# Attention whose score and maximum tiles share PSUM banks, with two maximum tiles directly in front of the value product

## The chip, the cores and the metric

One NeuronCore of a Trainium2 chip runs the whole program. The metric is the device time of one execution in microseconds (us); lower is better. Three executions of the kernel before gave 2846.3, 2852.3 and 2852.42 us, a median of 2852.3 us.

## The reference

A transformer block over x of 4 batches x 2048 tokens x 256 features, float32. It is a layer norm, then causal attention (16 heads of width 16 over 4 key and value heads, so 4 query heads share each) plus a soft mixture of experts (dispatch, 16 experts, combine), both added to the residual:

```python
q = (x @ wq.T).reshape(b, s, NKV, GS, HD)
k = (x @ wk.T).reshape(b, s, NKV, HD)
v = (x @ wv.T).reshape(b, s, NKV, HD)
att = jnp.einsum('bsgmd,btgd->bgmst', q, k) / scale
att = jnp.where(causal, -jnp.inf, att)
att = jax.nn.softmax(att, axis=-1)
ctx = jnp.einsum('bgmst,btgd->bsgmd', att, v).reshape(b, s, DIM)
x = x + ctx @ wo.T + ffn(x)
```

The change touches the attention alone.

## The kernel before, in words

The program is six stages one behind the other: prepare, project, attend, dispatch, experts, combine. `attend` takes about 1610 us of the span, from 280 us (its first exponential) to 1892 us.

**The work of attend.** It has 16 groups (4 batches x 4 key heads), and each group has four chunks c of 512 queries. A group is cut into 40 units, a unit being one block of 128 keys against one chunk for the group's 4 query heads. Of the 40 units 16 lie on the causal diagonal and need only the last 512, 384, 256 or 128 queries of the chunk (four units of each width); the other 24 are 512 wide. There is one step per unit, 640 in all; a step is named here by its position 0 to 39 in its group. In a step the tensor engine (PE) fills, in this order:

- four **score tiles** s0 to s3 (L742), one for each head, keys on the partitions, as wide as the unit. ScalarE (ACT) takes the exponential of each into `pr` (L665), and GpSimd (POOL) zeroes what lies above the diagonal (L642).
- four **maximum tiles** x0 to x3 (L755), queries on the partitions, from which VectorE (DVE) takes row maxima (L692 for full tiles, L698 with the causal mask for tiles on the diagonal, which are 128 to 512 wide). They work 22 steps ahead (`LEAD`), since the maxima must be inside the query operand before its scores are made.
- the **value product** (L781), four products side by side into the bank `acc`, of the unit two steps back (`AV_LAG`), as wide as that unit.

Scores and maxima of even heads use the lower 64 rows of the array, of odd heads the upper 64, so neighbours in the order can run together.

**Events.** Once per chunk there are two more tiles in the middle of a step. An **m event**: DVE reduces the maxima (L725), POOL splits them in two parts (L651, L653), PE turns them (L761), DVE copies them out (L706), and SyncE (SP) writes them by DMA into two rows of the query operand (L613). The first score tile of that chunk waits for it (L739). A **c event**: ACT copies the finished `acc` (L672), two steps later PE turns it back (L769), DVE takes reciprocals of the sums (L712) and multiplies (L716), and SP writes the context out (L619).

**What sets the order.** `program(s)` lists a step's fills by hand. All fills but the value product go into a ring of seven PSUM banks (`NBANK`), one fill to a bank in turn, so the fill n waits (`wait_bank`, L577) until its reader has let go of fill n-7. With eight fills in a step the fourth maximum x3 waits for the exponential of s0 of the same step:

```python
out = [st[0], xs[0], st[1], xs[1]] + ev + [xs[2], st[2], st[3], xs[3]] + av
bank_of = {e: n % NBANK for n, e in enumerate(fills)}
before = {e: fills[n - NBANK] for n, e in enumerate(fills) if n >= NBANK}
```

SP's queue holds, in program order, the loads of q, k and v of a later group (13 DMAs of 2.5 MB together, L590 to L592), the rows of the m events and the context of the c events. Loads of later groups stand at step 2 of groups 1 to 12; those of the first batch stand at the steps of `FIRST_LOADS` (0, 16 and 56 counted from the first score step).

## Time and profile before

| what | value |
|---|---|
| median of 3 executions | 2852.3 us (2846.3 to 2852.42) |
| the profiled execution's own time | 2859.1 us |
| its span, first to last instruction | 2857.4 us |
| mean granted TensorE clock | 0.963 |
| busy in the span: PE / DVE / ACT / POOL | 92% / 74% / 56% / 13% |
| one group of attention in the middle | 99.5 us |
| first, second group | 115.6 us, 111.4 us |

A profile row of a busy engine gives its start, its duration, the engine and line, and in brackets how long that engine had been idle and what ended it. PE is shown twice: PE is the product, PEld the load of its weights, which marks when an instruction was issued. A chain of waits is read best from PEld, since the busy share of PE includes pipelined time.

### The profile page before, as it was taken

Reading aid. Unit: us, or ns where it says so; the run is one execution under the profiler, and the core shown is the slowest. Engines: PE = TensorE matmul, PEld = TensorE weight load, DVE = VectorE, ACT = ScalarE, POOL = GpSimd, SP = SyncE. Lnnn points to the kernel's source line nnn. Section 1 sums busy time; section 2 is a strip of 40 time slices with the busy share of each in tenths; the row PEclk is TensorE's granted clock in tenths of the full one; section 3 lists DMA queues with packets and bytes.
Section 4 is the critical chain, followed back from the end, with each engine's and each line's share of the span. In section 5 each row is a group of like instructions: output and inputs, shape, how many; then the busy total and the mean of one; then the engine's idle time right before and its main releaser. Section 6 shows DMA issues by size and latency. Waiting matters only on the chain. (4 is left out here: it accounts for less than half of the span.)

```text
span 2857.4 us, 48019 instructions
## 1 busy us (share of the span) xinstructions
PE 2641.5 (92%) x16291; PEld 1580.7 (55%) x16291; DVE 2106.9 (74%) x5086; ACT 1605.1 (56%) x3282; POOL 382.9 (13%) x520
## 2 busy tenths in 40 slices
PE   4776999999999999999999999989989989969999
PEld 2443444444444444444444444447778868869999
DVE  6878787999999999899999989838465522226665
ACT  1440676777777777777777777766364431112221
POOL 1224110111111011111101111114130100030000
PEclk9985799999999999999999999999999999989999
DMA  3995333330332133023203000025344337656554
GB/s 118 311 309 66 47 44 43 44 44 11 41 44 32 18 44 44 14 37 44 37 13 44 8 7 7 7 100 206 109 165 140 103 102 252 199 167 191 193 193 152
DMA packets 200057, 268.13 MB, mean 94 GB/s; under 512 B 67076, under 2 KB 147080, under 8 KB 198312
## 3 DMA queue, kind: packets, MB, share of 16 engines
q1 hardware_dynamic: 179080, 245.56, 34.6%
q10 hardware_dynamic: 20768, 19.93, 2.2%
q8 instruction: 113, 1.85, 0.3%
q14 instruction: 96, 0.79, 0.1%
HBM read 163.55 MB, written 100.70 MB: 92 GB/s over the span
## 5 line engine op out<-in xcount | busy, mean ns | idle before, releaser
L665 ACT ACTIVATE att_pr<-att_ring 128x512 f32<-128x512 f32 (+3 forms) x2560 | 1173.8, 548 | 468.2 <-PE att_ring L742 461.1
L692 DVE TENSOR_REDUCE att_mx<-att_ring 128x1 f32<-128x512 f32 x1536 | 960.7, 682 | 82.2 <-PE att_ring L755 80.2
L755 PE MATMUL att_ring<-att_ks,att_qs 48*128 48x512 f32 (+3 forms) x2560 | 891.2, 441 | 59.5 <-DMA att_v<-v_rows 33.9
L742 PE MATMUL att_ring<-att_qs,att_ks 64*128 64x512 f32 (+3 forms) x2560 | 784.8, 411 | 15.2 <-DMA att_qs<-att_mrow 10.5
L742 PEld LDWEIGHTS att_ring<-att_qs,att_ks 64*128 64x128 f32 x2560 | 416.6, 188 | 559.6 <-DVE att_mx L692 249.1
L781 PE MATMUL att_acc<-att_pr,att_v 128*32 128x512 f32 (+3 forms) x5120 | 608.9, 548 | 4.2 <-issue 2.0
L755 PEld LDWEIGHTS att_ring<-att_ks,att_qs 48*128 48x128 f32 x2560 | 421.5, 191 | 251.2 <-ACT att_pr L665 145.9
L698 DVE CUSTOM_DVE_ANT_0 att_junk<-att_ring,w_causal 128x512 bf16<-128x512 f32 (+3 forms) x1024 | 465.9, 487 | 70.8 <-PE att_ring L755 51.9
L642 POOL TENSOR_SCALAR_AFFINE_SELECT att_pr<-att_pr 128x512 f32<-128x512 f32 x256 | 163.0, 637 | 1200.4 <-ACT att_pr L665 1200.4
L1075 PE MATMUL dis_ps<-dis_y,dis_lg 128*128 128x257 f32 x1024 | 226.6, 382 | 10.4 <-DMA dis_y<-y_rows 5.6
L1075 PEld LDWEIGHTS dis_ps<-dis_y,dis_lg 128*128 128x128 f32 x1024 | 194.7, 191 | 40.4 <-DMA dis_y<-y_rows 6.8
L1279 ACT CAST com_e1h<-com_tp 128x1024 fp32r<-128x1024 f32 x64 | 64.5, 1015 | 267.7 <-PE com_tp L1352 236.7
L781 PEld LDWEIGHTS att_acc<-att_pr,att_v 128*32 128x32 f32 x5120 | 101.3, 108 | 147.1 <-ACT att_pr L665 90.6
L1370 PE MATMUL com_mp<-com_eoh,com_e1h 128*128 x512 | 146.4, 286 | 5.2 <-DVE com_e1l L1304 5.2
L1370 PE MATMUL com_mp<-com_eol,com_e1h 128*128 x512 | 145.9, 285 | 0.0
L1370 PE MATMUL com_mp<-com_eoh,com_e1l 128*128 x512 | 145.9, 285 | 0.0
L884 ACT ACTIVATE dis_lg<-dis_lg 128x512 f32<-128x512 f32 x128 | 71.4, 633 | 102.0 <-DVE dis_lg L939 102.0
L1057 PE MATMUL dis_ps<-w_seTh,dis_yTh 128*128 128x512 f32 x256 | 104.4, 408 | 21.1 <-ACT dis_lg L914 12.3
L973 DVE TENSOR_REDUCE dis_nr<-dis_lg 128x1 f32<-128x1024 f32 x64 | 77.9, 1218 | 55.3 <-ACT dis_lg L914 55.3
L1161 DVE SCALAR_TENSOR_TENSOR exp_h<-exp_up,w_buT,exp_gate 128x256 f32<-128x256 f32 x64 | 28.0, 479 | 107.2 <-ACT exp_gate L1151 107.2
L914 ACT COPY dis_lg<-dis_ps 128x1024 f32<-128x1024 f32 x64 | 64.9, 1014 | 73.7 <-PE dis_ps L1057 73.6
L1151 ACT ACTIVATE exp_gate<-exp_gp,w_bgT 128x256 f32<-128x256 f32 x64 | 26.9, 471 | 139.8 <-PE exp_up L1191 139.8
(134 smaller groups left out, 2851.1 us busy)
## 6 DMA issues: line engine op xcount, KB each, us to landing
slot_exps<-dis_e SPq DMA_DIRECT2D x64, 512.0 KB, 2.8
com_e<-slot_exps SPq DMA_DIRECT2D x64, 512.0 KB, 3.5
att_qs<-q_parts SPq DMA_DIRECT2D x96, 256.0 KB, 10.2
q_parts<-proj_part SPq DMA_DIRECT2D x32, 512.0 KB, 4.1
dis_y<-y_rows SPq DMA_DIRECT2D x32, 512.0 KB, 3.8
att_ks<-k_parts SPq DMA_DIRECT2D x96, 128.0 KB, 11.1
y_rows<-proj_y SPq DMA_DIRECT2D x16, 512.0 KB, 4.5
y_cols<-proj_yT SPq DMA_DIRECT2D x16, 512.0 KB, 5.2
```

The lines of the kernel that those rows point to most:

```text
L642: nc.gpsimd.affine_select(out=blk, in_=blk, compare_op=ALU.is_ge, fill=0.0, base=0, pattern=[[0, GS], [1, P]], channel_multiplier=-1).then ...
L665: nc.scalar.activation(pr[:, s % NPR, h, off:CH], ring[:, bank_of["s", s, h], off:CH], ACT.Exp, scale=float(HD) ** -0.5).then_inc(exp_done, 1)
L692: nc.vector.tensor_reduce(dst, ring[:, bank, :], AX.X, ALU.max).then_inc(mb_used, 1)
L698: nc.vector.tensor_tensor_reduce(junk[:, h % 2, 0:wd], ring[:, bank, 0:wd], w["causal"][:, CH - wd:CH], 1.0, LOW, ALU.add, ALU.max, dst).t ...
L742: nc.tensor.matmul(ring[:, bank_of[e], off:CH], ks[r, g, kb * P:(kb + 1) * P], qs[r, g, c, hf * CH + off:(hf + 1) * CH], start=True, stop= ...
L755: nc.tensor.matmul(ring[:, bank_of[e], 0:wd], qs[r, g, c, q0:q0 + P], ks[r, g, j * CH:j * CH + wd], start=True, stop=True).then_inc(mb_rea ...
L781: last = nc.tensor.matmul(acc[VW * h:VW * (h + 1), off:CH], v[:, bg % NKV, kb, :], pr[:, n % NPR, h, off:CH], start=(n % NU in first), sto ...
L884: nc.scalar.activation(cols, cols, ACT.Exp).then_inc(d_ready, 1)
L973: nc.vector.tensor_reduce(nr[:, b % 2, t:t + 1], lg[:, b % 2, t, :], AX.X, ALU.max, negate=True).then_inc(nr_ready, 1)
L1057: last = nc.tensor.matmul(ps[:, i % 2, 2 * (t % 2) + h, :], lhs[:, n % RING, k, (t % TPC) * P:(t % TPC + 1) * P], w[rhs][:, k, h * 512:(h ...
L1075: last = nc.tensor.matmul(ps[:, i % 2, q, 0:D + 1], lg[:, b % 2, t, (hf * HB + q) * P:(hf * HB + q + 1) * P], y[:, m % 2, t % TPC, 0:D + 1 ...
L1370: last = nc.tensor.matmul(mp[:, q, 0:D], lhs[:, q, s, :], rhs[:, b, s, :], start=(s == 0 and rhs is eoh and lhs is e1h), stop=(s == SB - 1 ...
```

## The change

All in `attend`. A new function `place` puts fills into banks: a fill joins a bank that was opened at most four fills ago if it is of the same kind (scores of the same step and the same parity of head, or maxima of the same parity) and fits beside what is there. The tensor engine waits, when it opens a bank, for all that the bank held seven banks ago, and a reader waits for the last fill that shares its bank. The step's order is new. The c event's result is copied by ACT from PSUM to a new buffer `cc` after the second exponential of the step; DVE takes the reciprocals one step later, from `cc`, behind its first maximum; POOL multiplies. The reduction of an m event also stands behind the first maximum of the next step, and m events come one step later (`M_LAG` 3). The diagonal maxima come in another order, and the first loads stand earlier.

```diff
-        diag = [(c, h, t, c) for t in (3, 0, 2, 1) for h in heads]
-        if rg == 0:
-            diag = diag[len(diag) // 2:] + diag[:len(diag) // 2]
+        diag = [(c, h, t, c) for h in heads for t in (1, 3, 2, 0)]
...
-    M_LAG = 2
+    M_LAG = 3
...
-    FIRST_LOADS = {0: 1, 16: 2, 56: 3}
+    FIRST_LOADS = {-6: 1, 6: 2, 46: 3}
...
-        out = [st[0], xs[0], st[1], xs[1]] + ev + [xs[2], st[2], st[3], xs[3]] + av
+        out = [st[0], xs[0], xs[1], st[1]] + ev + [st[2], st[3], xs[2], xs[3]] + av
...
+    def place(fills):
+        held = [[] for _ in range(NBANK)]
+        where, before, mates, part, taken = {}, {}, {}, [], 0
+        for n, e in enumerate(fills):
+            need = width(e)
+            half = e[0], {"s": lambda: (e[1], e[2] % NRG), "x": lambda: MAXES[e[1] % NM][1] % NRG}.get(e[0], lambda: n)()
+            part = [p for p in part if n - p[2] <= NEAR]
+            spot = next((p for p in part if p[3] == half and CH - p[1] >= need), None)
+            if spot is None:
+                spot = [taken % NBANK, 0, n, half]
+                part = [p for p in part if p[0] != spot[0]] + [spot]
+                taken += 1
+                before[e], held[spot[0]] = held[spot[0]], []
+            where[e] = spot[0], spot[1]
+            held[spot[0]].append(e)
+            mates[e] = held[spot[0]]
+            spot[1] += need
+        return where, before, {e: m[-1] for e, m in mates.items()}
...
+    NEAR = 4
...
-                            sp.wait_ge(mb_used, turn[e] + 1)
+                            sp.wait_ge(cn_ready, bg * CPB + c + 1)
...
+                    for bg, c in c_events(s, C_LAG + 1):
+                        m = bg * CPB + c
+                        pool.wait_ge(rz_ready, m + 1)
+                        if bg >= 1:
+                            pool.wait_ge(c_out[c], 16 * bg)
+                        nc.gpsimd.tensor_tensor(cn[:, c].rearrange("p t (h d) -> p t h d", h=GS),
+                                                cc[:, c % 2, :, :, 0:HD],
...
-                            act.wait_ge(sT_ready, GS * s + h + 1)
+                            act.wait_ge(sT_ready, GS * s + last_mate["s", s, h][2] + 1)
...
+                            if h == 1:
+                                keep(s)
...
-                            nc.vector.tensor_tensor(cn[:, c].rearrange("p t (h d) -> p t h d", h=GS),
-                                                    ct[:, :, :, 0:HD],
```

**PE, a step with a 256 wide unit (position 34) and the beginning of the next**, in order of issue with the semaphores that each waits for; `att_ring` is the PSUM ring, `att_exp_done` counts exponentials, `att_mb_used` counts what DVE has read. Before:

```order
L742 MATMUL att_ring<-att_qs,att_ks 128x256 [waits att_mb_used]
L755 MATMUL att_ring<-att_ks,att_qs 128x512 [waits att_exp_done]
L742 MATMUL att_ring<-att_qs,att_ks 128x256 [waits att_mb_used]
L755 MATMUL att_ring<-att_ks,att_qs 128x512 [waits att_mb_used]
L755 MATMUL att_ring<-att_ks,att_qs 128x512 [waits att_exp_done]
L742 MATMUL att_ring<-att_qs,att_ks 128x256 [waits att_exp_done]
L742 MATMUL att_ring<-att_qs,att_ks 128x256 [waits att_mb_used]
L755 MATMUL att_ring<-att_ks,att_qs 128x512 [waits att_exp_done]
L781 MATMUL att_acc<-att_pr,att_v 32x512 [waits att_exp_done]
```

The last maximum, directly ahead of the value product, waits for an exponential, that of s0 of this step. The same step after the change:

```order
L808 MATMUL att_ring<-att_qs,att_ks 128x256 [waits att_mb_used]
L821 MATMUL att_ring<-att_ks,att_qs 128x512 [waits att_mb_used]
L821 MATMUL att_ring<-att_ks,att_qs 128x512 [waits att_exp_done]
L808 MATMUL att_ring<-att_qs,att_ks 128x256 [waits att_exp_done]
L808 MATMUL att_ring<-att_qs,att_ks 128x256 x2
L821 MATMUL att_ring<-att_ks,att_qs 128x512 [waits att_exp_done]
L821 MATMUL att_ring<-att_ks,att_qs 128x512 [waits att_mb_used]
L847 MATMUL att_acc<-att_pr,att_v 32x512 [waits att_exp_done]
```

s2 and s3 share the banks of s0 and s1 and wait for nothing; x3 now waits for a maximum of the step before, which DVE has read. In a step with 512 wide scores nothing is shared, and x3 still waits for s0 of its own step (three rows from such a step after the change: s3, x2, x3):

```order
L808 MATMUL att_ring<-att_qs,att_ks 128x512 [waits att_mb_used]
L821 MATMUL att_ring<-att_ks,att_qs 128x512 [waits att_mb_used]
L821 MATMUL att_ring<-att_ks,att_qs 128x512 [waits att_exp_done]
L847 MATMUL att_acc<-att_pr,att_v 32x512 [waits att_exp_done]
```

**SP, behind the load of a later group at step 2** (before, then after; `att_cn` is the context, `att_mrow` the rows of an m event):

```order
L592 DMA att_v<-v_rows 128x4x128
L613 DMA att_qs<-att_mrow 2x8x128 [waits att_mb_used]
L613 DMA att_qs<-att_mrow 2x8x128
L619 DMA context<-att_cn 128x4x64 [waits att_mb_used] x3
```

```order
L631 DMA att_v<-v_rows 128x4x128
L658 DMA context<-att_cn 128x4x64 [waits att_cn_ready]
L652 DMA att_qs<-att_mrow 2x8x128 [waits att_mb_used]
L652 DMA att_qs<-att_mrow 2x8x128
L658 DMA context<-att_cn 128x4x64 [waits att_cn_ready] x2
```

The rows of the m event for the third chunk, which were directly behind the load, are now behind one context write too.

## Rows read from the trace of the kernel before

**Rows 1.** The page's first part, and the granted clock in 40 slices

```profile
PE 2641.5 (92%) x16291; PEld 1580.7 (55%) x16291; DVE 2106.9 (74%) x5086; ACT 1605.1 (56%) x3282; POOL 382.9 (13%) x520
...
PEclk9985799999999999999999999999999999989999
```

**Rows 2.** Windows of groups 0, 1, 3, 14: PE, PEld, DVE, ACT, POOL, clock, DMA, GB/s

```profile
280.40:396.00 115.60, 108.85 (x646) 48.30 (x646) 92.98 (x246) 75.14 (x164) 11.88 (x24) 0.83 0.30 36
396.00:507.40 111.40, 102.53 (x664) 45.14 (x661) 91.44 (x241) 75.34 (x165) 11.88 (x24) 0.92 0.43 54
608.00:707.50 99.50, 97.61 (x664) 42.28 (x661) 91.22 (x241) 75.05 (x165) 11.88 (x24) 1.00 0.26 33
1703.00:1802.40 99.40, 97.59 (x662) 42.30 (x660) 91.25 (x241) 74.99 (x165) 11.86 (x24) 1.00 0.03 7
```

**Rows 3.** Timeline of PEld: a full step, then position 38 (128 wide), 39

```profile
794.12 0.18 PEld L742 LDWEIGHTS att_ring<-att_qs,att_ks 64*128 64x128 f32 x1 [0.84 <-DVE att_mx L692]
...
795.36 0.18 PEld L755 LDWEIGHTS att_ring<-att_ks,att_qs 48*128 48x128 f32 x1 [0.32 <-ACT att_pr L665]
795.79 0.16 PEld L781 LDWEIGHTS att_acc<-att_pr,att_v 128*32 128x32 f32 x8 [0.24 <-issue]
796.78 0.18 PEld L742 LDWEIGHTS att_ring<-att_qs,att_ks 64*128 64x128 f32 x1 [0.84 <-DVE att_mx L692]
...
797.37 0.19 PEld L742 LDWEIGHTS att_ring<-att_qs,att_ks 64*128 64x128 f32 x1
...
801.69 0.18 PEld L742 LDWEIGHTS att_ring<-att_qs,att_ks 64*128 64x128 f32 x1 [0.84 <-DVE att_mx L692]
...
802.44 0.18 PEld L755 LDWEIGHTS att_ring<-att_ks,att_qs 48*128 48x128 f32 x1
802.87 0.16 PEld L781 LDWEIGHTS att_acc<-att_pr,att_v 128*32 128x32 f32 x8 [0.24 <-ACT att_pr L665]
```

**Rows 4.** Timeline of ACT in the same stretch

```profile
794.72 2.06 ACT L665 ACTIVATE att_pr<-att_ring 128x512 f32<-128x512 f32 x4 [1.24 <-PE att_ring L742]
```

**Rows 5.** Groups by line and form, 608 to 1802.4 us (12 groups)

```profile
L692 DVE TENSOR_REDUCE att_mx<-att_ring 128x1 f32<-128x512 f32 x1153 | 721.1, 682 | 50.7 <-PE att_ring L755 49.0
...
L755 PEld LDWEIGHTS att_ring<-att_ks,att_qs 48*128 48x128 f32 x1920 | 304.0, 184 | 154.5 <-ACT att_pr L665 114.9 <-DVE att_mx L692 23.5 <-issue 4.0
...
L716 DVE TENSOR_TENSOR att_cn<-att_ring,att_rz 128x256 f32<-128x256 f32 x48 | 20.4, 424 | 1.7
...
L712 DVE RECIPROCAL att_rz<-att_ring 128x16 f32<-128x16 f32 x48 | 12.3, 257 | 5.3
```

**Rows 6.** Waits, 325 to 362 us (group 0), then 440 to 475 us (group 1)

```profile
PEld att_ring L742 <- DMA att_qs<-att_mrow: 6.3, 1, 6.3
...
PEld att_ring L742 <- DMA att_qs<-att_mrow: 6.0, 1, 6.0
```

**Rows 7.** Windows of ten us around those waits (granted clock: third number from the end)

```profile
350.00:360.00 10.00, 6.59 (x34) 3.33 (x34) 3.85 (x12) 4.13 (x8) 0.00 (x0) 0.50 0.19 27
420.00:430.00 10.00, 7.98 (x48) 3.84 (x40) 7.00 (x15) 4.38 (x12) 1.27 (x2) 0.76 0.38 59
```

**Rows 8.** Timeline of SP, then of PEld, steps 2 to 12 of group 3

```profile
612.12 0.35 SPq L590 DMA_DIRECT2D att_qs<-q_parts  x1
...
617.63 0.42 SPq L592 DMA_DIRECT2D att_v<-v_rows  x1
618.10 1.28 SPq L613 DMA_DIRECT2D att_qs<-att_mrow  x2
...
636.89 0.18 PEld L742 LDWEIGHTS att_ring<-att_qs,att_ks 64*128 64x128 f32 x1 [0.41 <-issue]
```

**Rows 9.** The tile view of att_v (all loads), and DMA issues on the page

```profile
DMA to landing us min/median/max: 8.7/18.2/19.1
...
context<-att_cn SPq DMA_DIRECT2D x64, 128.0 KB, 2.1
```

**Rows 10.** The page's groups: a two-input product on POOL, 1024 wide

```profile
L1002 POOL TENSOR_TENSOR dis_yTl<-dis_yTl,dis_yTh 128x1024 fp32r<-128x1024 f32 x15 | 41.7, 2777 | 22.1 <-issue 21.1
```

**Rows 11.** Timeline of PEld in group 1, step 10

```profile
424.16 0.16 PEld L781 LDWEIGHTS att_acc<-att_pr,att_v 128*32 128x32 f32 x8 [2.31 <-issue]
```

More of the change, by code:

```diff
@@ L504, in attend @@
     last_max = [max(n for n, x in enumerate(MAXES) if x[0] == c) + 1 for c in range(CPB)]
-    ALL_STEPS = range(-LEAD, STEPS + C_LAG + 1)
+    ALL_STEPS = range(-LEAD, STEPS + C_LAG + 2)
     def unit(n):
@@ L532, in program, with width @@
         xs = xs + [None] * (MPS - len(xs))
-        out = [st[0], xs[0], st[1], xs[1]] + ev + [xs[2], st[2], st[3], xs[3]] + av
+        out = [st[0], xs[0], xs[1], st[1]] + ev + [st[2], st[3], xs[2], xs[3]] + av
         return [e for e in out if e]
+    def width(e):
+        if e[0] == "s":
+            return CH - unit(e[1])[3]
+        if e[0] == "x":
+            c, h, t, j = MAXES[e[1] % NM]
+            return CH if j < c else (t + 1) * P
+        return P if e[0] == "m" else CH
+    def place(fills):
[17 more added lines that the diff above has]
+    NEAR = 4
     fills = [e for s in ALL_STEPS for e in program(s) if e[0] != "a"]
-    bank_of = {e: n % NBANK for n, e in enumerate(fills)}
-    before = {e: fills[n - NBANK] for n, e in enumerate(fills) if n >= NBANK}
+    where, before, last_mate = place(fills)
     turn = {e: n for n, e in enumerate(e for e in fills if e[0] != "s")}
+    dve_turn = {e: n for n, e in enumerate(e for e in fills if e[0] in "xm")}
     with ExitStack() as ctx:
@@ L553, in attend @@
         cT = a.sb("cT", [P, 2, CH])
-        rz = a.sb("rz", [P, TPC, GS])
+        cc = a.sb("cc", [P, 2, TPC, GS, HD + 1])
+        rz = a.sb("rz", [P, 2, TPC, GS])
         cn = a.sb("cn", [P, CPB, TPC, GS * HD])
@@ L565, in attend, with spot @@
         (sT_ready, exp_done, mask_done, pv_done, mb_ready, mb_used, m_step, nm_ready,
-         cT_ready, rz_ready) = (
+         cT_ready, cc_ready, rz_ready, cn_ready) = (
             sem(n) for n in ("sT_ready", "exp_done", "mask_done", "pv_done", "mb_ready",
-                             "mb_used", "m_step", "nm_ready", "cT_ready", "rz_ready"))
+                             "mb_used", "m_step", "nm_ready", "cT_ready", "cc_ready", "rz_ready", "cn_ready"))
         NLD = NRG * (len(Q_PART) + len(K_PART)) + 1
         def wait_bank(pe, e):
-            if e in before:
-                kind = before[e][0]
-                if kind == "s":
-                    _, n, h = before[e]
-                    pe.wait_ge(exp_done, GS * n + h + 1)
-                else:
-                    pe.wait_ge(mb_used, turn[before[e]] + 1)
+            exps = [GS * x[1] + x[2] + 1 for x in before.get(e, ()) if x[0] == "s"]
+            rest = [dve_turn[x] + 1 for x in before.get(e, ()) if x[0] in "xm"]
+            kept = [x[1] * CPB + x[2] + 1 for x in before.get(e, ()) if x[0] == "c"]
+            if exps:
+                pe.wait_ge(exp_done, max(exps))
+            if kept:
+                pe.wait_ge(cc_ready, max(kept))
+            if rest:
+                pe.wait_ge(mb_used, max(rest))
+        def spot(e, rows=slice(0, P)):
+            bank, col = where[e]
+            return ring[rows, bank, col:col + width(e)]
         with nc.Block() as block:
@@ L657, in _, with keep @@
             def _(act):
+                def keep(s):
+                    for bg, c in c_events(s, C_LAG):
+                        m = bg * CPB + c
+                        act.wait_ge(mb_ready, turn["c", bg, c] + 1)
+                        if m >= 2:
+                            act.wait_ge(cn_ready, m - 1)
+                        nc.scalar.copy(cc[:, c % 2], spot(("c", bg, c)).rearrange("p (t h w) -> p t h w", t=TPC, h=GS)
+                                       [:, :, :, 0:HD + 1]).then_inc(cc_ready, 1)
                 for s in ALL_STEPS:
@@ L679, in _, with row_maxes, inverse_sums @@
                     nc.vector.memset(ks[r, 0].bitcast(F32), 0.0).then_inc(zeroed[0], 1)
+                def row_maxes(s):
+                    for bg, c in m_events(s):
+                        m = bg * CPB + c
+                        dve.wait_ge(mb_used, dve_turn["x", maxes_of(s)[-1]] + 1)
+                        if m >= 1:
+                            dve.wait_ge(nm_ready, m)
+                        nc.vector.tensor_reduce(nm[:], mx[:, c % 2, :, 0:c + 1], AX.X, ALU.max,
+                                                negate=True).then_inc(nm_max, 1)
+                def inverse_sums(s):
+                    for bg, c in c_events(s, C_LAG + 1):
+                        m = bg * CPB + c
+                        dve.wait_ge(cc_ready, m + 1)
+                        if m >= 2:
+                            dve.wait_ge(cn_ready, m - 1)
+                        nc.vector.reciprocal(rz[:, c % 2], cc[:, c % 2, :, :, HD]).then_inc(rz_ready, 1)
                 for s in ALL_STEPS:
+                    if not maxes_of(s):
+                        row_maxes(s - 1)
+                        inverse_sums(s)
                     for e in program(s):
-                        if e[0] in ("s", "a"):
+                        if e[0] in ("s", "a", "c"):
                             continue
-                        n, bank = turn[e], bank_of[e]
+                        n = turn[e]
                         if e[0] == "x":
@@ L768, in _ @@
                             for t in range(TPC):
-                                last = nc.tensor.transpose(ring[:, bank_of[e], t * P:(t + 1) * P],
+                                last = nc.tensor.transpose(spot(e)[:, t * P:(t + 1) * P],
                                                            cT[:, c % 2, t * P:(t + 1) * P], w["ident"][:])
```

53 lines of the change are left out of this document (21 added, 32 removed).

## The prediction

> **What bounds the kernel now.** I read the page first. PE is busy 92% of the span, but its products are pipelined, so that share proves little; the reader should see that the clock is low only in the slices before 430 us [rows 1]. Only attend is touched, so I cut it into its groups by windows: a group in the middle takes 99.5 us, the first two 115.6 and 111.4 [rows 2]. In a middle group DVE is busy 91.2 us, ACT 75. DVE is close to the bound without being it.
>
> Next the timeline of weight loads for one full step [rows 3]. s0 is issued at 794.12, the last maximum x3 at 795.36 (+1.24), the value product at 795.79 (+0.43), the next s0 at 796.78 (+0.99): 2.66 us. The first piece is a wait: ACT begins the exponential of s0 at 794.72, four take 2.06 us [rows 4], so the first is done at about 795.3, and x3, whose bank it frees, goes at once. So the **chain is s0, its exponential, x3, value product, next s0**. The wait of maxima for ACT is the largest that maxima have, 114.9 us in 12 groups, against 23.5 for DVE [rows 5].
>
> Each piece shrinks with its width. For 128 wide scores the first piece is 0.75 (801.69 to 802.44, [rows 3]); I interpolate 1.08 for 384 and 0.92 for 256. Over 40 steps: 28 x 1.24 + 4 x (1.08 + 0.92 + 0.75) = 45.7 us. The second piece is 0.43, and I take 0.32 for the 12 steps whose x3 is narrow: 15.9. The third, by proportion 0.77, 0.55 and 0.28 for narrow units: 28 x 0.99 + 4 x 1.60 = 34.1. Together **95.7 of the 99.5 us**; the other 3.8 are steps where DVE, the events or ACT's extra copies last longer.
>
> **The change, part by part.** *Sharing.* A 512 wide score shares with nothing, so in 33 of 40 steps x3 waits as before for an exponential of its own step or for something as late; their 1.24 stays. In seven steps (256 wide: positions 9, 19, 34; 128 wide: 1, 11, 22, 38) x3 no longer does. PE could then issue it about 0.60 us after s0, where the seventh fill went in an unhindered step (796.78 to 797.37, [rows 3]). That saves 3 x 0.32 + 4 x 0.15 = 1.6 us a group. At position 19 two maxima also share a bank with the next step's, and DVE cannot read them until those are written: I take 0.1 back. 1.5 remains. The bounds are 0 (DVE or ACT is late there anyway) and 2.5 (x3 also finds less queue ahead).
>
> *Order of a step.* x2 stands behind s3 and no longer before s2. It is issued with x3 at the latest, 1.24 after s0, and DVE has x0 and x1 to read until about then (2 x 0.62 us: four maxima on DVE take 2.48). So no gain and no loss; if DVE had run dry at x2, it would cost up to 0.2 in each full step.
>
> *The c event.* DVE loses the product (0.424), its waits (0.15), and reads its reciprocals from SBUF: about 0.6 us less, four times a group, 2.4 us [rows 5]. DVE is not on the chain, so most of this buys nothing. What it buys is in steps 3 and 4, where an m and a c event fell in one step and now fall in two: I take 0.4. ACT gets a copy of 272 columns, about 0.4 us, behind its second exponential; a full step leaves ACT 2.66 - 2.06 = 0.6 idle, which covers it. POOL gets the product of 256 columns: a quarter of the 2.78 us of a 1024 wide one, 0.7 us [rows 10], with 88% of POOL's time idle and the next diagonal mask two steps from its use. If that cover went, four times 0.7 would be the cost, 2.8 a group.
>
> The Trainium skill (GPSIMD Engine Reference, 4.1 Engine selection) advises against this move: two-input elementwise work is about twice as slow there as on VectorE. By that the product would be 0.85 us in place of 0.7, which the same idle time hides; the row and the rule agree in size here.
>
> Sum for an undisturbed group: -1.5 - 0.4 = **-1.9 us**.
>
> *SP's queue.* In groups 1 to 12 a load of 2.5 MB is issued in step 2 and the m rows for the third chunk behind it; step 12 cannot begin without them. Load issued 612.12, its last DMA 617.63, landing 18.2 (median) to 19.1 later [rows 8, 9], so about 24 us after the load began, and the m rows hardly later. Step 12 came at 636.89, 24.77 after. Slack under 1 us. After the change the steps between are 0.9 us shorter (sharing at 9 and 11, events), and one context write of 128 KB is ahead of the m rows. At the load's own rate (2.5 MB in 24 us) that is 1.2 us; alone it lands in 2.1 with its start [rows 9]. So step 12 would wait 0.7 to 2.0 us. I take **1.0 us, in 12 groups**: between the ends, since the median landing is the shorter one. Behind SP's new wait for the context only these rows are queued, and they have eight steps.
>
> *First loads.* In group 0 and 1 PE stood 6.3 and 6.0 us for m rows that were behind a first load [rows 6], and the clock fell to 0.50 of full (1.2 GHz) right after [rows 7]. The loads now stand 15 steps, some 37 us, ahead of those rows, longer than the 24 us of a load. Group 0 is 16.1 over a middle group, of which 8.5 are its first eight steps at the low clock, which stay; 7.6 go. Group 1 is 11.9 over, of which I keep 4.3 at steps 10 to 12, a stall in issue [rows 11] and the low clock behind it; 7.6 go. Together **-15.2 us**.
>
> *The end.* The last context passes ACT, DVE and POOL in place of DVE alone: +0.4 + 0.7 - 0.4 and two hand-overs, **+1.2 us**.
>
> **Sum.** Groups 1 to 12: 12 x (1.9 - 1.0) = 10.8. Groups 0, 13, 14: 5.7. The last group has maxima in 18 steps only: 0.8. So 17.3 + 15.2 - 1.2 = 31.3 us less. The profiled execution took 2859.1 us, 6.8 above the median, so 2827.8 for it and 2852.3 - 31.3 = **2821 us** as the median.
>
> **Rivals.** *A, the chain opens further.* All 3.8 us above the chain vanish too, since DVE is lighter by 2.4, and step 12 does not wait. A group is then about 94 to 95.5: 15.4 x 4 to 5, with the first loads 77 to 90 us less, 2762 to 2775. For it: DVE waits 49.0 us for its reductions' tiles in 12 groups [rows 5], which is supply and could improve with two tiles in store during the value product. Against: nothing in the full steps moves x3. Chance 0.12.
>
> *B, only the first loads pay.* The sharing steps save nothing, because the next full step begins its exponential no earlier (ACT still busy), and step 12 eats the rest: 15 less, 2838. Chance 0.22.
>
> *C, slower: the mates' wait.* In a shared step ACT may not read s0 before s2 is written. In the Trainium skill (PSUM — Partial Sum Buffer, Terms) two engines on one bank at once are an error, not a stall, so this wait cannot be left out. The traces decide what it costs: if s2 comes more than 0.8 us behind s0, four 256 wide exponentials (1.2 us) end after the next s0 is ready, and ACT becomes late for the full step behind. Unhindered, s2 goes by 0.4 us. If DVE is late and it goes at 1.3, each of seven steps costs 0.5 more than before: 7 x 0.5 x 15.4 = 54, with -15.2 + 1.2 and 12 us at step 12 it is +52, 2904. A milder form, 0.25 a step, gives +25, 2877. Chance 0.12.
>
> *D, no change.* Two loads now stand back to back in group 1 (steps 2 and 6) and keep the DMA engines full for 45 us. The stall of 2.31 us in issue came under such a load [rows 11]; three or four more, each with the low clock behind it, and step 12 at its worse end (2.0) would take back the first loads' gain. Net within 8 us. Chance 0.09.
>
> **Chances and range.** The forecast (20 to 45 us less) has 0.45, A 0.12, B 0.22, C 0.12, D 0.09. A change of 0.3%, 8.6 us, is about what a measurement of this kernel tells from none. Faster: 0.45 + 0.12 + 0.22 = 0.79; same: 0.09; slower: 0.12. The range is from 2780 (half way to A, and the upper bound of sharing without the wait at step 12: 15 x 2.9 + 14 = 58, plus what DVE gives) to 2842 (B with one lost stall): it leaves out C, most of A and D.
>
> **What would show it.** Right: middle groups of 98.4 to 98.8 us with loads and 97.6 without; positions 9, 11, 34 and 38 shorter by 0.15 to 0.3; a wait of the first score tile for the m rows of about 1 us in step 12, in twelve groups; x3 at 1.24 after s0 in full steps; no wait of 6 us at 345 and 450 us; groups 0 and 1 near 107 and 103. Wrong: a first piece under 1.2 us in full steps (A), shared steps no shorter (B), ACT's idle time gone and its exponentials ending after the next s0 (C).

## The result, and the profile after

The changed kernel takes **2809.6 us** (median of four runs, 2807.3 to 2816.2) against 2852.4 for the kernel before on the same chip: ratio 0.9856, 95% interval 0.9832 to 0.988, 41 us less (34 to 48). Forecast were 2821 us and a range of 2780 to 2842. The profiled execution of the changed kernel took 2807.3 us, its span is 2805.6. The profiled one of before was above its median, this one is below, so the two traces differ by 51.8 us.

The page's first part and the granted clock, which answer to [rows 1]:

```profile
PE 2580.9 (92%) x16291; PEld 1540.1 (55%) x16291; DVE 2072.7 (74%) x5022; ACT 1610.7 (57%) x3346; POOL 417.8 (15%) x584
...
PEclk8995899999999999999999999999999999989999
```

DVE lost 34 us of work, POOL gained 35, ACT 6. Windows of groups 0, 1, 3 and 14, with the columns of [rows 2]:

```profile
280.50:382.60 102.10, 99.67 (x646) 42.89 (x645) 91.35 (x243) 74.95 (x167) 13.56 (x27) 0.92 0.35 43
382.60:482.30 99.70, 95.79 (x663) 40.61 (x661) 89.11 (x237) 75.45 (x169) 14.23 (x28) 0.98 0.48 60
580.20:678.30 98.10, 94.66 (x663) 40.18 (x661) 89.10 (x237) 75.51 (x169) 14.23 (x28) 1.00 0.26 34
1658.10:1755.70 97.60, 94.54 (x663) 40.34 (x661) 89.04 (x237) 75.49 (x169) 14.23 (x28) 1.00 0.03 7
```

Groups 0 and 1 are 13.5 and 11.7 us shorter, a group in the middle that loads 1.4, one that does not 1.8. Attention as a whole, from the first exponential to the last, one row of before and one of after:

```profile
280.50:1888.60 1608.10, 1564.52 (x10457) 675.58 (x10456) 1414.78 (x3707) 1199.55 (x2623) 189.10 (x380) 0.98 0.23 30
```

```profile
280.60:1838.50 1557.90, 1506.19 (x10461) 636.90 (x10464) 1379.41 (x3643) 1204.65 (x2686) 226.18 (x443) 0.99 0.24 32
```

So 50.2 of the 51.8 us are in here. I use this stretch below to set the experiments side by side. The timeline of weight loads shows a full step (position 28 of group 7) and then position 38, whose scores are 128 wide, as [rows 3] did:

```profile
1039.30 0.18 PEld L808 LDWEIGHTS att_ring<-att_qs,att_ks 64*128 64x128 f32 x1 [0.84 <-DVE att_mx L781]
...
1040.55 0.18 PEld L821 LDWEIGHTS att_ring<-att_ks,att_qs 48*128 48x128 f32 x1 [0.45 <-ACT att_pr L723]
1040.92 0.16 PEld L847 LDWEIGHTS att_acc<-att_pr,att_v 128*32 128x32 f32 x8 [0.19 <-issue]
1041.91 0.18 PEld L808 LDWEIGHTS att_ring<-att_qs,att_ks 64*128 64x128 f32 x1 [0.84 <-DVE att_mx L781]
```

```profile
1064.10 0.18 PEld L808 LDWEIGHTS att_ring<-att_qs,att_ks 64*128 64x128 f32 x1 [0.84 <-DVE att_mx L775]
...
1064.56 0.19 PEld L821 LDWEIGHTS att_ring<-att_ks,att_qs 48*128 48x128 f32 x2
1064.99 0.16 PEld L847 LDWEIGHTS att_acc<-att_pr,att_v 128*32 128x32 f32 x8 [0.24 <-issue]
```

In the full step x3 still waits for the exponential and comes 1.25 us after s0, the next s0 0.99 after the product. At position 38 both last maxima go without any wait, 0.46 us after s0. This is where sharing pays. Where it costs is position 20, in these rows of PEld, then of DVE (group 7):

```profile
1019.10 0.18 PEld L808 LDWEIGHTS att_ring<-att_qs,att_ks 64*128 64x128 f32 x1 [0.84 <-DVE att_mx L781]
...
1020.82 0.18 PEld L821 LDWEIGHTS att_ring<-att_ks,att_qs 48*128 48x128 f32 x1 [0.77 <-DVE att_mx L781]
1021.16 0.18 PEld L821 LDWEIGHTS att_ring<-att_ks,att_qs 48*128 48x128 f32 x1 [0.16 <-DVE att_mx L781]
1021.59 0.16 PEld L847 LDWEIGHTS att_acc<-att_pr,att_v 128*32 128x32 f32 x8 [0.25 <-issue]
```

```profile
1019.81 0.29 DVE L781 CUSTOM_DVE_ANT_0 att_junk<-att_ring,w_causal 128x128 bf16<-128x128 f32 x1 [0.71 <-issue]
...
1020.33 0.42 DVE L781 CUSTOM_DVE_ANT_0 att_junk<-att_ring,w_causal 128x256 bf16<-128x256 f32 x1
```

The two 128 wide maxima of position 19 share with the 256 wide ones of position 20. DVE, idle for 0.71 us, may not read them until these are written, and x2 and x3 of position 20 want the same two banks. The position lasts 3.49 us; its product starts 2.49 after s0.

The waits for m rows, over the whole run, and SP's queue in group 7:

```profile
PEld att_ring L808 <- DMA att_qs<-att_mrow: 13.4, 12, 1.9
```

```profile
982.32 3.75 SPq L652 DMA_DIRECT2D att_qs<-att_mrow  x2
```

Twelve waits, the largest 1.9 us. From the start of the first row write's issue to the end of the second's it is 3.75 us, where it was 1.28 in [rows 8].

### The profile page after: what moved, and what is told of

The parts are those of the page before. It is cut to its first block and busy times, and to the rows that moved or that the text cites. A ratio compares the mean times of both kernels' runs of the same rounds, so it can differ in the third digit from the quotient of the medians.

```text
span 2805.6 us, 48143 instructions
## 1 busy us (share of the span) xinstructions
PE 2580.9 (92%) x16291; PEld 1540.1 (55%) x16291; DVE 2072.7 (74%) x5022; ACT 1610.7 (57%) x3346; POOL 417.8 (15%) x584
## 5 line engine op out<-in xcount | busy, mean ns | idle before, releaser
L821 PE MATMUL att_ring<-att_ks,att_qs 48*128 48x512 f32 (+3 forms) x2560 | 853.7, 429 | 80.5 <-DMA att_v<-v_rows 34.5
L808 PE MATMUL att_ring<-att_qs,att_ks 64*128 64x512 f32 (+3 forms) x2560 | 621.5, 408 | 7.6 <-DMA att_qs<-att_mrow 7.5
L808 PEld LDWEIGHTS att_ring<-att_qs,att_ks 64*128 64x128 f32 x2560 | 327.8, 187 | 516.7 <-DVE att_mx L775 216.0
L821 PEld LDWEIGHTS att_ring<-att_ks,att_qs 48*128 48x128 f32 x2560 | 389.5, 189 | 279.4 <-ACT att_pr L723 141.5
L781 DVE CUSTOM_DVE_ANT_0 att_junk<-att_ring,w_causal 128x256 bf16<-128x256 f32 (+3 forms) x1024 | 466.8, 487 | 82.2 <-PE att_ring L821 53.2
```

The lines of the kernel that those rows point to most:

```text
L781: nc.vector.tensor_tensor_reduce(junk[:, h % 2, 0:wd], spot(e), w["causal"][:, CH - wd:CH], 1.0, LOW, ALU.add, ALU.max, dst).then_inc(mb_u ...
L808: nc.tensor.matmul(spot(e), ks[r, g, kb * P:(kb + 1) * P], qs[r, g, c, hf * CH + off:(hf + 1) * CH], start=True, stop=True).then_inc(sT_re ...
L821: nc.tensor.matmul(spot(e), qs[r, g, c, q0:q0 + P], ks[r, g, j * CH:j * CH + wd], start=True, stop=True).then_inc(mb_ready, 1)
```

## The experiments

There is one profile of each; "attention" is the stretch above. The kernel before was measured again beside the experiments, on the same chip, and each ratio is to that, so the ratios compare better than the medians. The lengths of positions here are from one step's first exponential to the next's, means over groups 4 to 11 unless a group is named. In a step whose scores share, the first exponential waits until s2 is written too, so this measure counts the beginning of that step to the one ahead of it. Where the text says "at the weight loads", the length is from the load of one step's s0 to that of the next, also as a mean over groups 4 to 11. Unless said otherwise the edit is to the changed kernel.

| kernel | median us | ratio to before | attention us |
|---|---|---|---|
| before | | 1 | 1608.1 |
| e1_first_loads | 2838.5 | 0.9952 (0.9931 to 0.9973) | 1586.8 |
| e2_no_sharing | 2829.8 | 0.9916 (0.9897 to 0.9934) | 1580.0 |
| the change | 2809.6 | 0.9856 (0.9832 to 0.988) | 1557.9 |
| e9_old_order | 2807.9 | 0.9855 (0.9839 to 0.987) | 1554.6 |
| e3_ctx_after_rows | 2809.2 | 0.9835 (0.9815 to 0.9855) | 1557.5 |
| e6_load_later | 2804.3 | 0.9837 (0.9823 to 0.9852) | 1553.9 |
| e4_x3_after_product | 2845.0 | 0.9981 (0.9969 to 0.9992) | 1601.6 |
| e5_x2x3_after_product | 2877.3 | 1.0093 (1.0076 to 1.011) | 1624.5 |
| e10_split_product | 3198.1 | 1.1218 (1.12 to 1.1236) | 1946.3 |
| e12_half_columns | 2747.7 | 0.9632 (0.9609 to 0.9654) | 1492.7 |
| e11_alternating | 2794.0 | 0.9788 (0.9772 to 0.9805) | 1540.2 |

### Which part pays

**e1**, the kernel before with one line changed:

```diff
-    FIRST_LOADS = {0: 1, 16: 2, 56: 3}
+    FIRST_LOADS = {-6: 1, 6: 2, 46: 3}
```

> The kernel before with the new first-load table and nothing else. Theory (each part pays where it acts): the first three loads land earlier in the program, group 0 of the trace shortens by 5 to 9 us and group 1 by 5 to 9 us, every later group keeps its 99.5 us; the time is 2835 to 2842 us. Rival (the lighter VectorE or the shared banks gave most of the 25 us of groups 0 and 1): both groups stay within 3 us of before and the time is above 2847 us.

Measured: 2838.5 us, by the ratio 14 less (8 to 20). Groups 0 and 1:

```profile
280.40:384.00 103.60, 102.00 (x645) 45.29 (x645) 92.66 (x246) 74.79 (x164) 11.87 (x24) 0.91 0.32 40
384.00:486.20 102.20, 99.15 (x664) 42.66 (x661) 91.16 (x241) 74.98 (x164) 11.86 (x24) 0.98 0.47 58
```

The place is as the theory has it, and a middle group keeps its 99.5. The size in the trace is larger, 11.9 and 9.2 us. About 4.3 us of group 0 is in its first eight steps (28.7 us before, 24.4 here), where the clock came back earlier: in the ten us from 290.5 and the ten from 300.5 us the granted clock was 0.50 and 0.57 before, and 0.62 and 1.00 in e1. These are the same windows of the change and of e4, which has the change's load table:

```profile
290.50:300.50 10.00, 9.94 (x59) 3.95 (x57) 8.44 (x20) 7.44 (x17) 1.27 (x2) 0.70 0.48 67
300.50:310.50 10.00, 9.96 (x76) 4.08 (x68) 9.42 (x23) 7.67 (x18) 1.89 (x3) 1.00 1.03 117
```

```profile
290.50:300.50 10.00, 10.00 (x45) 4.32 (x47) 7.41 (x16) 6.42 (x13) 1.27 (x2) 0.50 0.60 79
300.50:310.50 10.00, 9.91 (x64) 4.35 (x57) 6.92 (x18) 5.86 (x14) 1.25 (x2) 0.83 1.07 117
```

The granted clock (third number from the end) is at half, 0.50, in the ten us ahead of these in all four, and the load table alone does not fix when it returns: 0.50 and 0.83 in e4, 0.70 and 1.00 in the change. With one profile of each I can't say whether these 4 us belong to the load table or to the execution. The traces give 21 us where the medians give 14; but the profiled execution of before was 6.8 us above its median and that of e1 2.5 below.

**e2**, the change without sharing:

```diff
-    NEAR = 4
+    NEAR = -1
```

> The changed kernel with sharing of banks switched off (every tile has a bank of its own), everything else as it is. Theory: positions 9, 11, 34 and 38, where a narrow maximum tile now takes the other half of a bank, go back to what they last without a half tile (position 9 from 1.45 to about 2.2 us, 11 from 1.9 to 2.4, 34 from 1.67 to 2.3, 38 from 1.70 to 2.3), position 20 falls from 3.5 towards 2.7; a middle group lasts 1.2 to 1.8 us more and the time is 2825 to 2838 us. Rival (what pays is the work taken off VectorE at the c and m events, or the order of the narrow tiles): a middle group changes by under 0.4 us and the time is 2806 to 2815 us.

Measured: 2829.8 us, 20.2 more than the change, 17 by the ratios. Most middle groups are at 99.0 or 99.1, positions 9, 34 and 38 at 2.25, 2.45 and 2.34 us (with sharing 1.45, 1.67, 1.70), position 11 in groups that do not wait for rows at 1.92 (with sharing 1.28), position 20 at 2.67.

Part of what these lengths show lies in how they are counted. Position 34 of group 7 at the weight loads, without sharing and then with it, and last ScalarE's row with it:

```profile
1062.81 0.18 PEld L808 LDWEIGHTS att_ring<-att_qs,att_ks 64*128 64x128 f32 x1 [0.84 <-DVE att_mx L781]
...
1063.73 0.18 PEld L821 LDWEIGHTS att_ring<-att_ks,att_qs 48*128 48x128 f32 x1 [0.26 <-ACT att_pr L723]
```

```profile
1054.75 0.18 PEld L808 LDWEIGHTS att_ring<-att_qs,att_ks 64*128 64x128 f32 x1 [0.84 <-DVE att_mx L781]
...
1055.21 0.20 PEld L821 LDWEIGHTS att_ring<-att_ks,att_qs 48*128 48x128 f32 x2
```

```profile
1055.58 1.21 ACT L723 ACTIVATE att_pr<-att_ring 128x256 f32<-128x256 f32 x4 [0.77 <-PE att_ring L808]
```

Without sharing x3 waits for the exponential and comes 0.92 us after s0; with it, it comes at about 0.47, behind x2. But ScalarE's first exponential then begins 0.83 us after s0's load and not 0.48, since s2 has to be written first. By the exponentials position 34 is 0.8 us shorter and position 33, ahead of it, 0.35 longer. At the weight loads position 34 is 0.44 shorter (2.34 to 1.90) and position 33 is 2.61 us both times.

VectorE is busy for 89.4 us in group 3 here, 89.1 in the change: 1.8 less than in [rows 2], and that with the new order is worth 0.5 us a group. So it is the banks that pay, not the lighter VectorE.

**e9**, the step order of before in the change:

```diff
-        out = [st[0], xs[0], xs[1], st[1]] + ev + [st[2], st[3], xs[2], xs[3]] + av
+        out = [st[0], xs[0], st[1], xs[1]] + ev + [xs[2], st[2], st[3], xs[3]] + av
```

> The changed kernel with the step order of before (first score, first maximum, second score, second maximum, events, third maximum, third and fourth score, fourth maximum, product). Theory (the fourth maximum tile stays directly in front of the product, so a full step's chain is the same; the third maximum's place matters only for sharing): full steps stay at 2.66 to 2.67 us, a middle group changes by under 0.7 us, and the time is 2800 to 2820 us. Rival (two maximum tiles directly in front of the product give VectorE what it needs for the 0.9 us of the product): full steps last 2.75 us or more, VectorE idles behind each product, and the time is 2825 to 2860 us.

Measured: 2807.9 us; the intervals of the two cover each other almost wholly. The new order, with what it does to the sharing, is worth nothing that shows. The steps differ, their sum hardly does: position 20 falls from 3.49 to 2.68, while 9, 34 and 38 rise to 1.87, 2.02 and 2.06. The edit is more than an order, though: `place` looks back four fills, in the old order s2 is five behind s0, and so s0 and s2 no longer share, only s1 and s3 do; and the 128 wide maxima of position 19 come soon enough to share with the 384 wide ones of their own position. One bank saved is enough for x3: at the weight loads positions 34 and 38 are 1.90 and 1.88 us in both kernels, so their rise is in how they are counted, and only position 9 really rises, from 1.57 to 1.75. What two maxima in front of the product are worth with the sharing held as it is, no run shows.

### The wait for the m rows

**e3**, the context write behind the row writes on SP:

```diff
-                        elif e[0] == "c":
...
+                    for bg, c in c_events(s, C_LAG + 1):
...
```

> The changed kernel with SyncE's context write put behind the row writes of its step, so that no row write stands behind a context write in SyncE's queue. Theory (the row write of position 10 lands late because it is issued late behind a context write that stands behind the load): position 11 falls from 1.89 to 1.3 us in the twelve groups that load, as it is in the three groups that do not, and the time falls by 5 to 9 us, to 2800 to 2805 us. Rival (the row write is late because its bytes share the DMA engines with the 2.5 MB load): position 11 stays within 0.2 us and the time within 3 us of 2809.6 us.

Measured: 2809.2 us, no difference that can be told. Position 11 falls from a mean of 1.98 us in groups 1 to 12 to 1.69, against 1.28 without a wait. The waits stay twelve:

```profile
PEld att_ring L807 <- DMA att_qs<-att_mrow: 9.9, 12, 1.2
```

**e6**, the regular load three steps later, behind the rows:

```diff
-                    bg = (s - AV_LAG) // NU
-                    if s >= NU and (s - AV_LAG) % NU == 0 and bg + NKV - 1 < NBG:
+                    bg = (s - AV_LAG - 3) // NU
+                    if s >= NU and (s - AV_LAG - 3) % NU == 0 and bg + NKV - 1 < NBG:
```

> The changed kernel with the regular load issued at position 5 in place of 2, behind the row writes of that step. Putting these rows ahead of the context write alone shortened position 11 by only 0.2 to 0.3 us. Theory (the rows land late because their bytes queue behind the 2.5 MB of the load): position 11 lasts 1.28 us in all groups, the row writes are served before the load, and the time falls by 5 to 9 us, to 2800 to 2805 us. Rival (another row write or another wait takes its place, since the load now ends some 7 us later): position 12 or 24 grows by as much and the time stays within 3 us of 2809.6 us.

Measured: 2804.3 us. Position 11 is 1.28 in the groups with loads, none of the twelve waits for m rows is left (there is one of 1.4 us elsewhere, in front of position 24 of group 1), and group 3 takes 97.3:

```profile
577.60:674.90 97.30, 94.58 (x663) 40.39 (x661) 88.94 (x237) 75.54 (x169) 14.29 (x28) 1.00 0.26 34
```

So the rows were late behind the load. The context write ahead of them was a smaller part, 0.3 of 0.7 us. The gain in the time is 5 us by the medians and 4.0 by attention; the two intervals against before overlap, so it is the trace that carries this.

### What holds a full step

**e4**, x3 behind the product, and **e5**, x2 and x3 behind it:

```diff
-        out = [st[0], xs[0], xs[1], st[1]] + ev + [st[2], st[3], xs[2], xs[3]] + av
+        out = [st[0], xs[0], xs[1], st[1]] + ev + [st[2], st[3], xs[2]] + av + [xs[3]]
```

```diff
-        out = [st[0], xs[0], xs[1], st[1]] + ev + [st[2], st[3], xs[2], xs[3]] + av
+        out = [st[0], xs[0], xs[1], st[1]] + ev + [st[2], st[3]] + av + [xs[2], xs[3]]
```

> The changed kernel with the fourth maximum tile behind the value product instead of ahead of it. Theory (a full step is a chain: first score tile, its exponential which frees the bank, fourth maximum tile, value product, next first score tile): the exponential's bank no longer stands ahead of the value product, a full step falls from 2.66 us to VectorE's 2.45 to 2.55 us, a middle group from 98 to 91 to 95 us, and the time is 2715 to 2775 us. Rival (the four maximum tiles ahead of the value product keep VectorE supplied while TensorE works through the product of 0.86 us): the tile now arrives 0.9 us later than VectorE wants it, a full step lasts 2.66 us or more, and the time is 2805 to 2880 us.

> The changed kernel with the third and fourth maximum tiles both behind the value product. With the fourth alone behind it a full step stayed at 2.67 us, and there the third tile started 1.06 to 1.09 us into the step, when VectorE had read the fourth tile of the step before, and the product 0.43 us later. Theory (a new chain of the same length took over: fourth tile, its reading, third tile of the next step, product, fourth tile): with neither tile between them the product starts at about 0.7 us, full steps fall to VectorE's 2.5 us where VectorE has tiles in store, and the time is 2740 to 2800 us. Rival (two tiles in store do not last VectorE through the product of 0.9 us): VectorE idles 0.3 us or more in each full step, these last 2.7 us or more, and the time is 2820 to 2920 us.

Measured: 2845.0 and 2877.3 us, my theory missed both times. Position 28 of e4, then of e5:

```profile
1058.74 0.19 PEld L821 LDWEIGHTS att_ring<-att_ks,att_qs 48*128 48x128 f32 x2 [0.84 <-DVE att_mx L781]
...
1060.17 0.18 PEld L821 LDWEIGHTS att_ring<-att_ks,att_qs 48*128 48x128 f32 x1 [0.67 <-DVE att_mx L781]
1060.54 0.16 PEld L847 LDWEIGHTS att_acc<-att_pr,att_v 128*32 128x32 f32 x8 [0.19 <-issue]
1061.54 0.19 PEld L821 LDWEIGHTS att_ring<-att_ks,att_qs 48*128 48x128 f32 x2 [0.84 <-ACT att_pr L723]
```

```profile
1071.53 0.18 PEld L808 LDWEIGHTS att_ring<-att_qs,att_ks 64*128 64x128 f32 x1 [0.65 <-DVE att_mx L781]
1071.96 0.16 PEld L847 LDWEIGHTS att_acc<-att_pr,att_v 128*32 128x32 f32 x8 [0.25 <-issue]
1072.96 0.19 PEld L821 LDWEIGHTS att_ring<-att_ks,att_qs 48*128 48x128 f32 x2 [0.84 <-DVE att_mx L775]
```

With seven banks and eight tiles a step, the tile in front of the product needs the bank of the first tile behind the previous product. In the change these are x3 and s0 (ScalarE reads), in e4 x2 and x3, in e5 s3 and x2 (VectorE reads). The step from one product to the next stays a chain of one tile, its reading, a tile and the product. Through VectorE it is no shorter: the tile waits 0.67 and 0.65 us for it. Position 28 lasts 2.73 and 2.79 us (2.61 in the change), and a middle group 100 and 102 to 103. Both times came out in the range of the rival, that VectorE runs out of tiles during the product, and there is a sign of it in e5: between 600 and 1700 us VectorE waited 131.8 us for maximum tiles, against 73.8 in the change (in e4 51.5, but with 58.9 us of idle time for which the profile names no releaser, against 16.3). How much of the 35 and 68 us is the chain and how much VectorE's supply, these runs do not tell apart.

**e10**, the product in two halves of two heads (the waits stay with the first half, the release with the second):

```diff
-        out = [st[0], xs[0], xs[1], st[1]] + ev + [st[2], st[3], xs[2], xs[3]] + av
+        out = [st[0], xs[0], xs[1], st[1]] + ev + av[:1] + [st[2], st[3], xs[2], xs[3]] + av[1:]
...
-                            for h in range(GS):
+                            for h in range(2 * hp, 2 * hp + 2):
```

> The changed kernel with the value product cut in two: heads 0 and 1 in front of the third score tile, heads 2 and 3 at the end of the step. Nothing else moves. Theory (a full step is the chain first score, its exponential, fourth maximum tile 1.24 us after it, 0.43 us, product 0.99 us, next first score): only half of the product stands on the chain, which would last 2.2 us, so full steps fall to VectorE's 2.5 us, a middle group from 98 to 91 to 95 us, and the time is 2715 to 2775 us. Rival (a full step is set by how VectorE and ScalarE share seven banks, not by the product's place): full steps stay at 2.66 us and the time within 10 us of 2809.6 us.

Measured: 3198.1 us, a miss by 400 us, and worth the most. The 512 wide forms of the product's matmuls in the groups of the change, then of e10 (count, busy us, mean ns), and position 28 of e10:

```profile
L847 PE MATMUL att_acc<-att_pr,att_v 128*32 128x512 f32 x3584 | 480.0, 607 | 2.2 <-ACT att_cT L734 1.5 <-ACT att_pr L723 0.6
```

```profile
L848 PE MATMUL att_acc<-att_pr,att_v 128*32 128x512 f32 x3584 | 943.4, 605 | 16.5 <-ACT att_cT L734 14.9
```

```profile
1219.65 0.14 PEld L848 LDWEIGHTS att_acc<-att_pr,att_v 128*32 128x32 f32 x4 [0.37 <-issue]
1220.64 0.19 PEld L808 LDWEIGHTS att_ring<-att_qs,att_ks 64*128 64x128 f32 x2 [0.84 <-ACT att_pr L723]
...
1221.25 0.14 PEld L848 LDWEIGHTS att_acc<-att_pr,att_v 128*32 128x32 f32 x4 [0.31 <-issue]
1222.23 0.18 PEld L808 LDWEIGHTS att_ring<-att_qs,att_ks 64*128 64x128 f32 x1 [0.84 <-DVE att_mx L781]
```

The same 3584 instructions, each as long as before, cover twice the time: a half with two heads takes 0.98 to 0.99 us, as the whole does with four. The four heads write 32 partitions each of the same bank, and four take the time of two. The Trainium skill (TensorE: Matmul & The Clock Gate, "Why this matters for your kernels", small-M matmuls) says that outputs at different 32-partition slices are worked on at the same time, with 2.38 times for three tiles. This trace agrees that they run side by side; a product of three heads, or of one alone, no run here has. So e10 added a whole product to each step, and says nothing on the chain.

**e12** halves the columns of the product, so that the kernel leaves out half of every value product except at the first unit of each chunk; all other work stays:

```diff
+                            end = CH if n % NU in first else off + (CH - off) // 2
                             for h in range(GS):
-                                last = nc.tensor.matmul(acc[VW * h:VW * (h + 1), off:CH], v[:, bg % NKV, kb, :],
-                                                        pr[:, n % NPR, h, off:CH], start=(n % NU in first),
+                                last = nc.tensor.matmul(acc[VW * h:VW * (h + 1), off:end], v[:, bg % NKV, kb, :],
+                                                        pr[:, n % NPR, h, off:end], start=(n % NU in first),
```

> The changed kernel with the value product over half of its columns, except at the first unit of each chunk: the other half of the attention output is left out, all else stays. Cutting the product in two by heads gave 122 us a group, since each half took as long as the whole (four heads run side by side); this cut shortens it, from about 0.9 to about 0.45 us. Theory (the product stands on the chain of a full step, first score, exponential, fourth maximum tile, product, next first score): full steps fall from 2.66 to VectorE's 2.4 to 2.5 us, a middle group to 91.5 to 94.5 us, and the time is 2710 to 2765 us. Rival (full steps are held by the readers of the banks and the product lies beside them): full steps stay above 2.6 us and the time above 2790 us.

Measured: 2747.7 us, 62 less than the change. Position 28, and group 13, which does not load:

```profile
1005.30 0.18 PEld L808 LDWEIGHTS att_ring<-att_qs,att_ks 64*128 64x128 f32 x1 [0.41 <-issue]
...
1006.91 0.16 PEld L848 LDWEIGHTS att_acc<-att_pr,att_v 128*32 128x32 f32 x8 [0.18 <-issue]
1007.48 0.18 PEld L808 LDWEIGHTS att_ring<-att_qs,att_ks 64*128 64x128 f32 x1 [0.41 <-issue]
```

```profile
1504.40:1593.90 89.50, 86.57 (x664) 43.26 (x660) 87.16 (x237) 75.46 (x169) 14.20 (x28) 1.00 0.03 8
```

From product to next s0 it is 0.57 us in place of 0.99, and position 28 lasts 2.18 in place of 2.61. The product is on the chain, and the rival falls. Not all steps follow (position 6 stays at 2.66), and in the 89.5 us of group 13 VectorE is busy for 87.2, so it is close to being the bound. Group 13 is the shortest in the middle. Only it and group 7 (90.0 us) had a mean granted clock of 1.00; the others from group 1 to 14 had 0.89 to 0.96 and took 92.7 to 95.9 us. Waits for m rows are back too, twelve with 20.0 us together. So the time of the whole kernel shows less than what the shorter product gives a step.

### A faster version

**e11** puts scores and maxima strictly in turn, and keeps e6's load:

```diff
-        out = [st[0], xs[0], xs[1], st[1]] + ev + [st[2], st[3], xs[2], xs[3]] + av
+        out = [st[0], xs[0], st[1], xs[1]] + ev + [st[2], xs[2], st[3], xs[3]] + av
```

> The changed kernel with scores and maxima strictly in turn (s0 x0 s1 x1, events, s2 x2 s3 x3, product) and the regular load at position 5. The order of before inside the changed kernel gave the same time as its own, with other steps short and long: position 20 fell from 3.49 to 2.68 us, positions 9, 34 and 38 rose by 0.35 to 0.4 us. Theory (a tile waits for the reader of the tile that stood behind it a step earlier, so when the two readers take turns the waits in front of the product are shortest, and the half tile shares with a tile that comes soon): position 20 stays near 2.5 to 2.7 us and positions 9, 34, 38 under 1.8 us, a middle group lasts 96.0 to 96.8 us and the time is 2785 to 2797 us. Rival (the order within a step only moves waits about, the sum is set by the full steps): a middle group stays at 97.1 to 97.6 us and the time at 2801 to 2808 us.

Measured: 2794.0 us, ratio 0.9788; its interval lies below the change's, 19 us under it by the ratios, and below e6's, 14 us under that, which is what the order adds. Group 3, and position 20 of group 7:

```profile
574.90:671.40 96.50, 94.39 (x661) 40.60 (x660) 88.65 (x237) 75.53 (x170) 14.28 (x28) 1.00 0.26 34
```

```profile
1009.36 0.18 PEld L808 LDWEIGHTS att_ring<-att_qs,att_ks 64*128 64x128 f32 x1 [0.84 <-DVE att_mx L781]
...
1011.04 0.16 PEld L847 LDWEIGHTS att_acc<-att_pr,att_v 128*32 128x32 f32 x8 [0.24 <-ACT att_pr L723]
```

Here the 128 wide maxima of position 19 go into what is left of banks with 384 wide ones of the same position, and nothing has to wait for the next step: the product of position 20 starts 1.68 us after s0 and not 2.49. Positions 9, 34 and 38 keep their gain (1.44, 1.67, 1.71). That is 97.3 to 96.5 a group.

## Why the prediction was right, point by point

**Sign, range and bound.** Faster, inside the range, 11 us below the number. The bound was read rightly: x3 kept its place in full steps, and e12 shows that the product stands on that chain. What the text did not say is that the exponential is only one of several readers that can close it; e4 and e5 show the others.

**Sharing, -1.5 us a group.** Measured -1.7 to -1.8 (99.0 in e2 to 97.3 in e6, in groups where no m rows cost time). That the sum came so close is in part luck, since two terms were mis-sized and the errors nearly cancelled. Counted in group 7 at the weight loads, the seven shared steps save 2.7 us together where the prediction had 1.6: 0.57, 0.44 and 0.29 at positions 9, 34 and 38, for which it had 0.32, 0.32 and 0.15, because x3 comes 0.34 to 0.47 us after s0 there and not 0.60. Position 20 loses 0.8, of which the prediction had 0.1, and position 39 another 0.1. Those 0.8 are not the price of sharing as such: in e11, where these maxima share otherwise, positions 19 and 20 last 1.54 and 2.68.

**Order, -0; events, -0.4.** Both together, without sharing: 99.5 in before to 99.0 in e2, -0.5. They were not measured apart; e9 shows only that, with sharing on, the old order does no worse. The new instructions were sized well. The rows are POOL's product and ACT's copy in groups 3 to 14:

```profile
L689 POOL TENSOR_TENSOR att_cn<-att_cc,att_rz 128x256 f32<-128x256 f32 x48 | 29.8, 621 | 56.9 <-DVE att_rz L759 56.9
...
L713 ACT COPY att_cc<-att_ring 128x272 f32<-128x272 f32 x48 | 18.7, 390 | 0.0
```

0.62 for 0.7 forecast, 0.39 for 0.4. The Trainium skill's advice against such work on GpSimd (GPSIMD Engine Reference, 4.1 Engine selection: about twice as slow) did not matter: 621 ns here against 424 on VectorE before is 1.46 times, and neither VectorE nor ScalarE shows a wait for it between 600 and 1700 us.

**SP's queue, +1.0 in 12 groups.** The wait is there, in twelve groups, at position 12, 13.4 us in the waits. Position 11 grew by 0.7 each, 8.4 in sum: inside 0.7 to 2.0 only at its edge. The cause I gave, a context write ahead of the rows, was the lesser one (e3); the main one, rows behind the load in a program that has become shorter, is shown by e6.

**First loads, -15.2.** By the ratio of e1 -14 (8 to 20). In the traces group 0 lost 11.9 with the table alone and group 1 9.2. Both 6 us waits are gone. What was mis-sized is "which stay" and "of which I keep 4.3": the first eight steps at the low clock were shorter by 4 to 5 us, and steps 10 to 12 of group 1, 4.70, 2.95 and 3.84 before, are 2.73, 2.62 and 3.77, so one stall in issue did not come back. Both differ between kernels with one load table, each seen in one execution: e4's windows show it for the clock, and in e1 the long steps of group 1 stood at positions 10 and 14 (3.71 and 3.88 us).

**The end, +1.2, and the last group, -0.8.** The last group is 3.6 us shorter (86.4 to 82.8), 1.5 of it at its positions 26 and 27 (3.14 and 2.94 to 2.11 and 2.44), where a c event had DVE's product in the middle of short steps. I had costed the events only where two met. That the product is the reason is not shown: these positions stay as long in e1 (3.13 and 2.97) and are short in e2, e6 and e9, but they are long again in e4 (3.27 and 2.82) and e11 (2.61 and 4.36), where DVE has no such product either. From the last exponential to the end of the program it is 968.8 before and 967.3 after: the 1.2 us more do not show.

**Rivals.** A fell: full steps kept their length. B fell by e2: sharing does pay. C's wait is real, but it is not on the chain where C put it: the exponentials of a shared step begin 0.35 us later at position 34, and ScalarE is still idle for 0.46 us before those of position 35. Where a mate costs time it is maxima whose mates come a step later (position 20), 0.8 once a group, not 0.5 seven times. D fell: two loads back to back in group 1 left one long step, 3.77 us.

## What to carry to other kernels

Where tiles rotate over fewer banks than a step has tiles (here eight over seven), find the wait that repeats: the tile in front of the long instruction needs the bank of the first tile behind the last one. Moving tiles only changes which reader closes that loop, so shorten the long instruction or free a bank by sharing. When tiles share a bank, count from the first one's write to the last one's: a partner in the next step holds up both reader and successor. And small writes that others wait for belong ahead of a bulk load in a queue, which each gain elsewhere makes more pressing.

## What the runs showed of the hardware

Matmuls into four different slices of 32 output partitions of a bank took no longer than into two: halving the heads left 0.98 us of 0.99, while halving the columns brought 0.57. On SP's queue, issuing itself can slow down: behind 13 loads and a context write the two row writes took 1.67 and 2.03 us of issue, up to 4.24 over the run, and without the context write ahead of them 0.63 and 0.62, at most 0.75. In e6, where they stand ahead of the load, they took at most 0.75 too, but one context write behind two loads took 6.91. The tile view of the change, then of e3 (least, median and most of one, in ns):

```profile
L652 SPq DMA_DIRECT2D att_qs<-att_mrow x128: 610/616/4236, 249.4 to 1802.9; - x128
```

```profile
L652 SPq DMA_DIRECT2D att_qs<-att_mrow x128: 610/616/746, 249.4 to 1802.3; - x128
```

What holds up the issue there is not settled. Nor is why TensorE's granted clock rose to full at 290 to 310 us in one execution and later in that of another kernel with the same loads.
